# A selective scan in a hybrid layer stack: seven instead of five buffers for a step's feed and states

## The chip, the cores and the metric

The kernel runs on one core of a Trainium2 chip. The metric is the device time of one execution in microseconds (us): 3016.0 us, the median of three runs (3014.9 to 3018.98).

## What is computed

Four layers on x of shape (8, 512, 512): a selective scan (Mamba-like), a mixture of experts with a shared expert, causal attention, and a mixture of experts again. The change lies in the first one. Cut to it, the reference is

```python
xz = jnp.einsum('bld,kd->blk', x, W_x)             # x: layer-normed, 8 x 512 x 512
dt_raw, b_ssm, c_ssm = xz[..., :128], xz[..., 128:144], xz[..., 144:]
dt = jax.nn.softplus(jnp.einsum('blr,dr->bld', dt_raw, W_dt) + b_dt)
d_a = jnp.exp(dt[..., None] * a[None, None])       # 16 states for each channel
dbx = dt[..., None] * b_ssm[:, :, None, :] * x[..., None]
def step(h, inp):
    da_t, dbx_t, c_t = inp
    h = da_t * h + dbx_t
    y = jnp.einsum('bdn,bn->bd', h, c_t)
    return (h, y)
```

and after all four layers, each added to its input, the sum is the output. The experts' layer takes for each of 4096 tokens the best 6 of 64 experts, where an expert serves at most its first 64 tokens, and adds a shared gated expert of width 704.

## The kernel before

Everything is in float32. The five engines' programs are written from one plan, a list of items such as ("feed", k); each engine goes through the list and issues what is its own, so the order on an engine is that of the plan, and semaphores join the engines. Four stages follow each other: the scan (0 to about 1060 us), the first experts, attention, and the second experts.

**The scan stage.** One batch element has 512 time steps, which lie along the free axis, and 512 channels in four blocks of 128 partitions. A *step* k is one channel block and two of the 16 states (NG = 2): 32 steps a batch element, 256 in all (NSTEP). A step goes through the engines like this:

- `feed(k)`, POOL (GpSimd), L1872: writes dt*x*B for both states into buffer `hb[k % HB]`, 128x1024.
- `decay(k)`, ACT (ScalarE), L1720: writes exp(dt*a), one 128x512 tile for each state, into one of three PSUM banks.
- `scan(k)`, DVE (VectorE): two scans of 512 elements at L1349, then the product of the second state with C at L1358. In every eighth step (k % 8 == 4) DVE makes the first state's product too, L1355.
- `weigh_c(k)`, POOL, L1880: the product of the first state with C, in place in `hb`; left out in every eighth step.
- `sum(k)`, PE (TensorE), L1004: eight transposing 128x128 products add the step to y in a PSUM bank and signal `y_summed`. From then on `hb[k % HB]` is free.
- `x1(b, c)`, DVE, L1364: adds a finished y bank to x; it stands in the plan two steps after the block's last step, so it comes twice in a row every 16 steps.

The plan's order in step k is feed(k + 2), scan(k), weigh_c(k), x1 of step k - 2 where due, the work beside, sum(k - 1). AHEAD = 2 says how far the feeds run in front. C and B come from DRAM through three rotating buffers (NBC = 3, `bc_in`), broadcast to all partitions.

**The work beside.** In the same steps stand the preparation of the next batch element (norm, transposes, projections, softplus) and, for the batch element before, the first experts' norm, gate and routing and its shared expert: `sg` (L1054 on PE), `su` (L1075), `silu` (ACT, L1747), `hid` (DVE, L1377), `sd` (L1089 and L1095 on PE, L1392 on DVE). The products of PE go through a ring of three PSUM banks. An `sg` or `su` is one block of PE work that stands in front of a `sum` on PE's queue.

**The ring of buffers.** A feed may write its buffer when the step that used it last is summed:

```python
        if k >= HB:
            G.wait_ge(p.y_summed, k - HB)
        nc.gpsimd.tensor_tensor(out=p.hb[k % HB], ...)
```

With HB = 5 and the feed of step k + 2 standing in step k, POOL waits in step k until PE has summed step k - 3. What stands behind it on POOL's queue is weigh_c(k).

**The memory.** All tiles are cut by hand out of one SBUF tensor, `arena`, of ARENA words a partition. `hb` is the last part of `scan_memory`; the first experts' weights lie over the scan's tiles, and what lies behind starts at the end of `hb`. In front of `arena` lies the scratch in which the descriptors of DMAs issued by POOL are built. POOL issues these: 64 gathers (L1938), 64 accumulating writes of expert rows (L1948), and 12 accumulating writes of the shared expert (L1921), all behind the scan stage.

Of the kernel before, what the change touches and what calls it, by code (L numbers as in the profile page):

```python
# [33 lines left out]
NEG = -1e30  # L34
SCALE = float(1.0 / np.sqrt(np.float32(HEAD)))
BANK = 512
ARENA = 52928

# [3 lines left out]
GROUPS = NSTATE // NG  # L44
STEPS = GROUPS * HC
NSTEP = BATCH * STEPS
HB = 5
BOTH_EVERY, BOTH_AT = 8, 4
NBC = 3
AHEAD = 2  # L50
# [112 lines left out]
class Arena:  # L163
# [3 lines left out]
    def cut(self, shape, dt=FP32):  # L167
        n = int(np.prod(shape))
        words = n if dt in (FP32, I32) else (n + 1) // 2
        words = (words + 7) // 8 * 8  # L170
        assert self.at + words <= ARENA, (self.at, words)
        view = self.base[:, self.at:self.at + words]
# [30 lines left out]
def over(ap, axis, n):  # L203
    v = ap.unsqueeze(axis)
    shape = list(v.shape)
    shape[axis] = n
    return v.to_broadcast(shape)


def step_of(k):  # L210
    b, i = divmod(k, STEPS)
    pair, i = divmod(i, 2 * GROUPS)
    g, c = divmod(i, 2)
    return b, 2 * pair + c, g


def dve_weighs_both(k):
    return k % BOTH_EVERY == BOTH_AT
# [11 lines left out]
def block_of(ring, b, c):  # L230
    return half_of(ring, b, c // 2)[:, c % 2, :]
# [368 lines left out]
class Program:  # L600


    def __init__(self, nc, ctx, dram):
        self.nc, self.ctx, self.d = nc, ctx, dram
        self.signals = []
        base = ctx.enter_context(nc.sbuf_tensor("arena", [P, ARENA], FP32))
        self.bank = [ctx.enter_context(nc.psum_tensor(f"bank{i}", [P, BANK], FP32)) for i in range(8)]
# [117 lines left out]
    def scan_memory(self, sb):  # L725
# [10 lines left out]
        self.bc = [sb.cut([2, NG, SEQ]) for _ in range(NBC)]  # L736
        self.hb = [sb.cut([NG, SEQ]) for _ in range(HB)]

# [203 lines left out]
def tensor_engine(p, eng):  # L942
# [44 lines left out]
    def y_sum(k):  # L987
        b, c, g = step_of(k)
        s, w, each = b % 2, p.hb[k % HB], b * HC + c
        y = bank[Y_BANKS[c % 2]]  # L990
# [282 lines left out]
def vector_engine(p, eng):  # L1273
# [68 lines left out]
    def scan(k):  # L1342
        b, c, g = step_of(k)
        h = p.hb[k % HB]
        banks, both = [bank[p.da_bank(k, n)] for n in range(NG)], dve_weighs_both(k)
# [479 lines left out]
def pool_engine(p, eng):  # L1825
# [40 lines left out]
    def feed(k):  # L1866
        b, c, g = step_of(k)
        G.wait_ge(p.dtx_ready, b, c // 2)
        G.wait_ge(p.bc_in[k // 2 % NBC], k // 2)
        if k >= HB:  # L1870
            G.wait_ge(p.y_summed, k - HB)
        nc.gpsimd.tensor_tensor(out=p.hb[k % HB], in0=over(block_of(p.dtx, b, c), 1, NG), in1=p.bc[k // 2 % NBC][:, 0],  # L1872
                                op=ALU.mult).then_inc(*p.fed.up(k))
# [382 lines left out]
```

## Time and profile before

| | us |
|---|---|
| median of three runs | 3016.0 |
| the profiled execution | 3015.6 |
| its span on the core | 3013.8 |
| around the span | 1.8 |
| scan stage, to the last scan step's x1 | about 1060 |

The profile is of one execution. It gives each engine's busy time, what ended each idle stretch of an engine (the releaser), and the instructions in order of time. A stall of an engine that is not the last link costs nothing by itself. The rows that matter stand below, in groups.

### The profile page before, as it was taken

What the parts mean: (1) busy time and instruction counts of PE and PEld (TensorE: products, weight loads), DVE (VectorE), ACT (ScalarE), POOL (GpSimd) and SP (SyncE); (2) the same over time, 40 slices, a digit from 0 to 9 for tenths busy, and PEclk for the clock granted to TensorE, in tenths of its full rate; (3) what the DMA queues carried; (4) which work ended last, traced back from release to release, by engine and by line L of the source; (5) the groups of instructions that cost most, each with busy time, mean ns of one, the idle gap of its engine ahead of it and who ended that gap; (6) DMA issues with size and microseconds to landing.
All of it is one profiled execution on the core that took longest, in us unless ns stands there. A gap on an engine that the chain in (4) does not pass through costs nothing.

```text
span 3013.8 us, 37461 instructions
## 1 busy us (share of the span) xinstructions
PE 2720.2 (90%) x13484; PEld 1435.0 (48%) x13484; DVE 1772.6 (59%) x3835; ACT 1281.5 (43%) x2693; POOL 1483.1 (49%) x912
## 2 busy tenths in 40 slices
PE   4668888988889879999969999999899999999998
PEld 3454555545555534433335555555544444444443
DVE  5898999999899952222236666665624444222222
ACT  4657566665756411111127676666712220111111
POOL 5999989988998802222135555554500001121211
PEclk7779999999999889999989999999999999999999
DMA  5454555545554369999940000001135324899997
GB/s 187 153 184 154 185 167 166 187 142 195 166 176 164 131 265 358 396 393 393 392 121 1 29 29 29 29 29 42 64 100 189 118 79 159 308 381 338 359 337 218
DMA packets 168234, 566.13 MB, mean 188 GB/s; under 512 B 22832, under 2 KB 24752, under 8 KB 167536
## 3 DMA queue, kind: packets, MB, share of 16 engines
q1 hardware_dynamic: 149904, 521.65, 47.0%
q0 software_dynamic: 17088, 40.90, 5.9%
q8 instruction: 106, 1.74, 0.2%
q10 hardware_dynamic: 1056, 1.18, 0.1%
q14 instruction: 80, 0.66, 0.1%
HBM read 487.89 MB, written 75.79 MB: 187 GB/s over the span
## 4 chain that ended last, share of the span: by engine, by line
PE 53%; DVE 3%; ACT 2%; POOL 2%; DMA 2%; issue 1%; POOLq 0%; SPq 0%; DVEq 0%; ACTq 0%
PE bank L1151 10%; PE bank L1054 5%; PE bank L1075 5%; PE bank L1177 5%; PE bank L1089 5%; PE bank L1202 5%; PE bank L1259 4%; PE bank L1236 3%; PE bank L1224 2%; PE bank L1248 2%; POOL arena L1970 2%; DMA scratch_y<-arena 2%; PE bank L1134 1%; PE bank L1190 1%; ACT arena L1791 1%
## 5 line engine op out<-in xcount | busy, mean ns | idle before, releaser
L1872 POOL TENSOR_TENSOR arena<-arena 128x1024 f32<-128x1024 f32 x256 | 603.9, 2363 | 55.7 <-PE bank L1004 50.4
L1720 ACT ACTIVATE bank<-arena 128x512 f32<-128x512 f32 x512 | 344.5, 689 | 345.2 <-DVE arena L1349 184.7
L1970 POOL TENSOR_TENSOR arena<-arena 128x2048 f32<-128x2048 f32 (+3 forms) x128 | 296.9, 2323 | 275.0 <-DVE arena L1584 274.9
L1004 PE MATMUL bank<-arena 128*128 128x128 f32 x2048 | 296.7, 299 | 104.7 <-POOL arena L1880 103.5
L1791 ACT ACTIVATE arena<-arena 128x256 f32<-128x256 f32 (+3 forms) x512 | 287.1, 565 | 148.6 <-DVE arena L1575 124.9
L1349 DVE TENSOR_TENSOR_SCAN bank<-bank,arena 128x512 f32<-128x512 f32 x288 | 344.7, 1207 | 1.6 <-ACT bank L1720 1.1
L1004 PEld LDWEIGHTS bank<-arena 128*128 128x128 f32 x2048 | 258.0, 154 | 179.7 <-POOL arena L1880 128.5
L1151 PE MATMUL bank<-arena 128*64 128x352 f32 x2048 | 323.8, 470 | 0.0
L1054 PE MATMUL bank<-arena 128*128 128x512 f32 x640 | 298.2, 610 | 18.7 <-DVE arena L1377 18.7
L1075 PE MATMUL bank<-arena 128*128 128x512 f32 x640 | 288.7, 594 | 6.7 <-DVE arena L1339 6.7
L1880 POOL TENSOR_TENSOR arena<-arena 128x512 f32<-128x512 f32 x224 | 286.5, 1279 | 4.7 <-DVE arena L1349 4.5
L1349 DVE TENSOR_TENSOR_SCAN arena<-bank,arena 128x512 f32<-128x512 f32 x224 | 271.8, 1213 | 27.2 <-POOL arena L1872 14.5
L1089 PE MATMUL bank<-arena 128*128 128x512 f32 x640 | 286.5, 599 | 0.0
L1938 POOL DMA_INDIRECT arena<-scratch_xn,arena x64 | 68.7, 1073 | 440.8 <-DVE arena L1543 242.4
L1575 DVE CUSTOM_DVE_ANT_0 arena<-bank,arena 128x256 f32<-128x256 f32 (+3 forms) x512 | 220.9, 487 | 23.7 <-PE bank L1224 15.8
L1151 PEld LDWEIGHTS bank<-arena 128*64 128x64 f32 x2048 | 143.5, 139 | 147.6 <-issue 143.6
L1516 DVE TENSOR_TENSOR arena<-arena,bank 128x352 f32<-128x352 f32 x64 | 33.3, 521 | 306.9 <-issue 178.6
L1377 DVE TENSOR_TENSOR arena<-arena,bank 128x512 f32<-128x512 f32 x80 | 54.7, 683 | 244.5 <-PE bank L1075 243.7
L1075 PEld LDWEIGHTS bank<-arena 128*128 128x128 f32 x640 | 120.4, 190 | 160.2 <-issue 144.7
L1780 ACT ACTIVATE arena<-bank,arena 128x512 f32<-128x512 f32 x64 | 44.0, 687 | 346.7 <-PE bank L1177 324.2
L1054 PEld LDWEIGHTS bank<-arena 128*128 128x128 f32 x640 | 119.5, 195 | 149.9 <-issue 128.8
L1765 ACT ACTIVATE arena<-bank 128x352 f32<-128x352 f32 x64 | 29.7, 464 | 374.7 <-PE bank L1151 362.4
(145 smaller groups left out, 4187.9 us busy)
## 6 DMA issues: line engine op xcount, KB each, us to landing
arena<-scratch_bc SPq DMA_DIRECT2D x128, 1024.0 KB, 5.5
arena<-in_w_out SPq DMA_DIRECT2D x128, 768.0 KB, 15.3
arena<-in_w_gate SPq DMA_DIRECT2D x128, 704.0 KB
arena<-in_w_up SPq DMA_DIRECT2D x128, 704.0 KB
scratch_x<-arena SPq DMA_DIRECT2D x16, 1024.0 KB, 4.7
scratch_xn<-arena SPq DMA_DIRECT2D x15, 1024.0 KB, 4.6
arena<-scratch_x SPq DMA_DIRECT2D x44, 256.0 KB, 6.2
arena<-scratch_x SPq DMA_DIRECT2D x8, 1024.0 KB, 7.5
```

The costliest lines, as they stand in the source:

```text
L1004: i = nc.tensor.matmul(y[:, t * P:(t + 1) * P], w[:, n, t * P:(t + 1) * P], p.ident, is_transpose=True, start=False, stop=g == GROUPS - 1 ...
L1054: i = nc.tensor.matmul(out[:, :], f["swg"][:, c, j * P:(j + 1) * P], xnT[:, c, :], start=c == 0, stop=c == HC - 1)
L1075: i = nc.tensor.matmul(out[:, :], f["swu"][:, c, j * P:(j + 1) * P], xnT[:, c, :], start=c == 0, stop=c == HC - 1)
L1089: nc.tensor.matmul(out[:, :], f["shT"][:, j, t * P:(t + 1) * P], f["swd"][:, j, :], start=j == 0, stop=False)
L1151: i = nc.tensor.matmul(bank[1 + w][mine, 0:INTER], f["xeT"][k % 2][:, c, mine], f["ring"][(2 * k + half) % nw][w][:, c, :], start=c == 0, ...
L1349: nc.vector.tensor_tensor_scan(out=banks[n][:, :] if n or both else h[:, n, :], data0=banks[n][:, :], data1=h[:, n, :], initial=0.0, op0=A ...
L1575: nc.vector.tensor_tensor_reduce(out=p.sc[i % NSC][:, 0:width], in0=bank[c][:, 0:width], in1=p.amask[:, SEQ - width:], scale=-SCALE, scala ...
L1720: nc.scalar.activation(bank[p.da_bank(k, n)][:, :], block_of(p.dt, b, c), ACT.Exp, scale=p.alog[:, c, state:state + 1]).then_inc(*p.decaye ...
L1791: nc.scalar.activation(p.pr[n % 2][:, c, OFFSET[t]:OFFSET[t] + width], p.sc[i % NSC][:, 0:width], ACT.Exp, scale=-1.0, bias=p.nb[:, k % 2, ...
L1872: nc.gpsimd.tensor_tensor(out=p.hb[k % HB], in0=over(block_of(p.dtx, b, c), 1, NG), in1=p.bc[k // 2 % NBC][:, 0], op=ALU.mult).then_inc(*p ...
L1880: nc.gpsimd.tensor_tensor(out=h, in0=h, in1=p.bc[k // 2 % NBC][:, 1, 0, :], op=ALU.mult).then_inc(*p.weighted["pool"].up(k))
L1970: nc.gpsimd.tensor_tensor(out=own, in0=own, in1=over(p.rden[:, k % 2, :], 2, width), op=ALU.mult).then_inc(*p.divided.up(k))
```

## The change

`HB` goes from 5 to 7, and so does the distance in `feed`'s wait. Two buffers of 128x1024 words are 2048 words a partition more, so `ARENA` grows by 2048 words (8192 bytes). The descriptors' scratch is set to 8192 bytes a partition; it was not given before, and its default is 16384. With it `arena` begins 8192 bytes lower. AHEAD and NBC stay.

```diff
-ARENA = 52928
+ARENA = 52928 + 2048
+DYNAMIC_SCRATCH = 8192
...
-HB = 5
+HB = 7
...
-    nc = bacc.Bacc("TRN2", target_bir_lowering=False, num_devices=1)
+    nc = bacc.Bacc("TRN2", target_bir_lowering=False, num_devices=1, dynamic_dma_scratch_size=DYNAMIC_SCRATCH)
```

No instruction moves on any engine and none is added. What changes is in the waits. POOL's queue at the beginning of the scan steps, feeds (128x1024) and weighings (128x512) with the semaphores each waits on, of the kernel before:

```order
L1872 TENSOR_TENSOR arena<-arena 128x1024 [waits bc_in2]
L1880 TENSOR_TENSOR arena<-arena 128x512 [waits scanned]
L1872 TENSOR_TENSOR arena<-arena 128x1024 [waits y_summed]
L1880 TENSOR_TENSOR arena<-arena 128x512 [waits scanned]
L1872 TENSOR_TENSOR arena<-arena 128x1024 [waits y_summed,bc_in0]
L1872 TENSOR_TENSOR arena<-arena 128x1024 [waits y_summed]
```

and the same place with the change (lines are one further down):

```order
L1873 TENSOR_TENSOR arena<-arena 128x1024 [waits bc_in2]
L1881 TENSOR_TENSOR arena<-arena 128x512 [waits scanned]
L1873 TENSOR_TENSOR arena<-arena 128x1024
L1881 TENSOR_TENSOR arena<-arena 128x512 [waits scanned]
L1873 TENSOR_TENSOR arena<-arena 128x1024 [waits bc_in0]
L1873 TENSOR_TENSOR arena<-arena 128x1024 [waits y_summed]
```

The first feed that waits for a sum is the eighth, not the sixth, and each later one waits for a sum that lies two steps further back.

## Rows read from the trace of the kernel before

**Rows 1.** The page: the span, and part 1, busy us of each engine.
```profile
span 3013.8 us, 37461 instructions
PE 2720.2 (90%) x13484; PEld 1435.0 (48%) x13484; DVE 1772.6 (59%) x3835; ACT 1281.5 (43%) x2693; POOL 1483.1 (49%) x912
```

**Rows 2.** Busy time by stretches of the scan stage: length, PE, PEld, DVE, ACT, POOL, granted clock, DMA.
```profile
75.00:175.00 100.00, 57.99 (x287) 44.07 (x286) 88.25 (x99) 57.67 (x85) 99.38 (x62) 0.70 0.47 160
175.00:1020.00 845.00, 733.95 (x3352) 450.18 (x3351) 797.74 (x1060) 540.78 (x801) 767.27 (x456) 0.94 0.52 171
1018.00:1025.00 7.00, 6.12 (x14) 3.54 (x15) 6.86 (x7) 2.83 (x5) 6.87 (x5) 0.51 0.56 193
1025.00:1060.00 35.00, 34.55 (x141) 19.84 (x140) 25.82 (x30) 17.56 (x22) 23.59 (x14) 1.00 0.17 60
```

**Rows 3.** DVE's two largest waits, 175 to 1060 us: us, times, longest.
```profile
DVE arena L1364 <- PE bank L1004: 27.8, 8, 8.5
DVE arena L1349 <- ACT bank L1720: 12.4, 13, 2.0
```

**Rows 4.** DVE's waits for feeds, 0 to 175 us.
```profile
DVE arena L1349 <- POOL arena L1872: 14.5, 10, 4.9
```

**Rows 5.** POOL's waits before feeds, 75 to 1020 us.
```profile
POOL arena L1872 <- PE bank L1004: 49.2, 27, 4.2
POOL arena L1872 <- DMA arena<-scratch_bc: 2.0, 6, 0.5
```

**Rows 6.** Timeline around 284 and 415 us: start, us, instruction, [idle before <- releaser].
```profile
284.58 0.69 DVE L1364 TENSOR_TENSOR arena<-arena,bank 128x512 f32<-128x512 f32 x1 [3.01 <-PE bank L1004]
...
396.37 0.68 DVE L1377 TENSOR_TENSOR arena<-arena,bank 128x512 f32<-128x512 f32 x1
397.10 3.54 PE L1054 MATMUL bank<-arena 128*128 128x512 f32 x4 [2.67 <-DVE arena L1377]
...
413.37 1.91 PE L1004 MATMUL bank<-arena 128*128 128x128 f32 x16
414.56 2.36 POOL L1872 TENSOR_TENSOR arena<-arena 128x1024 f32<-128x1024 f32 x1 [4.22 <-PE bank L1004]
415.32 0.69 DVE L1364 TENSOR_TENSOR arena<-arena,bank 128x512 f32<-128x512 f32 x1 [4.42 <-PE bank L1004]
```

**Rows 7.** POOL's timeline, last quarter of the last batch element.
```profile
974.53 2.36 POOL L1872 TENSOR_TENSOR arena<-arena 128x1024 f32<-128x1024 f32 x1 [1.61 <-PE bank L1004]
980.84 2.35 POOL L1872 TENSOR_TENSOR arena<-arena 128x1024 f32<-128x1024 f32 x1 [2.72 <-PE bank L1004]
988.08 2.38 POOL L1872 TENSOR_TENSOR arena<-arena 128x1024 f32<-128x1024 f32 x1 [1.35 <-PE bank L1004]
...
1017.56 1.26 POOL L1880 TENSOR_TENSOR arena<-arena 128x512 f32<-128x512 f32 x1
1030.75 2.36 POOL L1872 TENSOR_TENSOR arena<-arena 128x1024 f32<-128x1024 f32 x1 [1.14 <-PE bank L1004]
```

**Rows 8.** DVE's timeline: scans of steps 242 and 245, and the first of the last x1.
```profile
1004.82 1.21 DVE L1349 TENSOR_TENSOR_SCAN arena<-bank,arena 128x512 f32<-128x512 f32 x1
...
1014.28 1.21 DVE L1349 TENSOR_TENSOR_SCAN arena<-bank,arena 128x512 f32<-128x512 f32 x1
...
1058.97 0.69 DVE L1364 TENSOR_TENSOR arena<-arena,bank 128x512 f32<-128x512 f32 x1 [8.48 <-PE bank L1004]
```

**Rows 9.** PE's timeline, the last 40 us of the scan stage.
```profile
1018.88 1.97 PE L1004 MATMUL bank<-arena 128*128 128x128 f32 x8 [3.72 <-POOL arena L1880]
1020.64 5.73 PE L1054 MATMUL bank<-arena 128*128 128x512 f32 x8
...
1029.63 2.78 PE L1004 MATMUL bank<-arena 128*128 128x128 f32 x24
...
1041.48 1.09 PE L1004 MATMUL bank<-arena 128*128 128x128 f32 x8 [0.45 <-POOL arena L1880]
```

**Rows 10.** DMAs issued by POOL: the page's queue, gathers' landing, first experts' row writes.
```profile
q0 software_dynamic: 17088, 40.90, 5.9%
```
```profile
DMA to landing us min/median/max: 6.6/7.1/11.2
```
```profile
L1948 POOL DMA_INDIRECT scratch_y<-arena x32: 1542/1587/1623, 1149.9 to 1522.0; - x32
```

## The prediction

> **What bounds the kernel now.** I read the page's first part, then the windows of the scan stage, the waits of DVE and of POOL in it, and the timelines at the stalls. PE is busy for 90% of the span and DVE for 59% [rows 1], but those are means over four stages, and only the first has the ring that is changed. In it, from 175 to 1020 us, DVE is busy for 797.74 of 845 us, 94%; POOL for 767.27, 91%; PE for 733.95, 87% [rows 2]. So DVE sets the pace, and what a change can give is what DVE idles. From 175 to 1060 us it idles before L1364, the x1, for a sum of PE (27.8 us, 8 times, the longest 8.5) and before its scans for a decay of ACT (12.4 us, 13 times) [rows 3]. No wait of DVE for a feed stands in that list. DVE waits for feeds earlier, 14.5 us up to 175 us [rows 4], where POOL is busy for 99.38 of 100 us [rows 2]: there POOL has too much work and does not wait for PE at all.
>
> POOL's wait for the ring is real: 49.2 us, 27 times, before a feed, for PE's sums [rows 5]. The question is whether anything that DVE waits for stands behind it.
>
> **The change part by part.** *The ring of seven.* The wait before a feed is for the sum five steps ahead of the one in hand, not three. A step takes about 4.1 us: the x1 stalls at 284.58 and 415.32 [rows 6] are one batch element apart, 130.7 us for 32 steps. So PE may fall behind by some 8 us more before POOL stops. The longest stall is 4.2 us [rows 5], so I take all 49.2 us as gone, and ask place by place who profits.
>
> First, the feeds themselves. They are two steps ahead of DVE and DVE waits for none of them after 175 us: 0 us.
>
> Second, weigh_c, which stands behind the feed on POOL, and through it PE's sums and then x1. DVE's stalls at x1 are eight, 27.8 us; the longest, 8.5 us, and one of 0.2 right behind it end the stage, and the six others, 19.1 us, look alike. At 415 us: `hid` ends on DVE at 396.37 + 0.68, and PE, which waited 2.67 us for just that, starts an sg at 397.10 [rows 6]. From there PE has work without a stop, sg, su and sums, and reaches the sum that x1 waits for at 413.37; DVE has stood for 4.42 us then, and POOL for 4.22 [rows 6]. Both wait for the same late PE. PE's row of work starts at an instant that DVE sets, so an earlier POOL moves nothing: x1 is as late as before. Only POOL's part of the double stall goes, and POOL then stands at weigh_c or the next feed, for DVE. The same holds at 284.58 (3.01 us) [rows 6] and at the other four: in each the last stop of PE ahead of its row of work is for DVE. 0 us of 19.1.
>
> Third, ACT's decays (12.4 us): the two largest kinds, 2.0 and 1.3 us, come where ACT has a softplus and a table change between decays. ACT waits for POOL there in no row: 0 us.
>
> Fourth, the end of the stage. The last stall at x1 is 8.48 us [rows 8], and here PE's row of work starts after a wait for POOL: 3.72 us at 1018.88 and 0.45 us at 1041.48, both for weigh_c; in between and behind PE is busy for 34.55 of 35 us [rows 2, 9]. PE was last held by POOL, so here POOL's delay counts. How much? POOL was stopped at 974.53, 980.84 and 988.08 for 1.61 + 2.72 + 1.35 = 5.68 us [rows 7], and from 988.08 to 1018.9 it never idles, so it carries a lag. It can lose that lag only down to DVE's scan. The weighing of step 242 can start when the scan does end, at 1004.82 + 1.21 = 1006.03 [rows 8]. From there POOL has a feed, a weighing and two feeds to the weighing of step 245: with 1.22 us from start to start for a weighing and 2.32 for a feed, 1006.05 + 1.22 + 2.32 + 1.22 + 2 x 2.32 = 1015.45. The scan of step 245 ends at 1014.28 + 1.21 = 1015.49 [rows 8]. So that weighing starts at about 1015.51 and not at 1017.56 [rows 7]: PE goes on 2.05 us earlier. The 5.68 us of stops are more than the lag that is to be lost, also with the earlier weighings held by their scans. At 1030.75 another stop of 1.14 us goes [rows 7], so the weighing that PE awaits at 1041.48 comes 2.05 + 1.14 = 3.2 us earlier, and PE's 0.45 us there go too. Sum for PE, and for the last x1, since nothing else is in its way: 2.05 + 0.45 = **2.5 us**. What follows (the last routing, the first gathers, the weights' loads, which wait for the last sum) starts from there and moves along.
>
> Bounds: if the clock does better the rest comes with it. PE's sg after the 3.72 us wait took 5.73 us for 8 products [rows 9] at a granted 0.51 [rows 2], the level of 1.2 GHz, against 3.60 for the same block at full level. With a shorter wait the level may stay up; then POOL's weighing of 1041 is the limit, and the gain 3.3 us. Above all stands the stall of 8.48 us [rows 8], which can't go twice. Below, 0, if PE meets the lower level elsewhere.
>
> *The bc loads.* Their buffers are given back by POOL's and DVE's weighings, not by PE. POOL waits 2.0 us for them in 945 us [rows 5]; some of POOL's gain may turn into this wait, which costs no one (same reason as above).
>
> *The scratch.* The software queue moves 17088 packets [rows 10] in 140 DMAs, 122 each. They all come after the scan stage, and a gather lands in 7.1 us, 11.2 at most [rows 10]. A gather is issued three expert pairs ahead of its use, and a pair takes (1522.0 - 1149.9)/31 = 12.0 us [rows 10]. If half the scratch held only one DMA at a time, the second and third gather at the start would land later by about 6 and 12 us; at 12 us a pair that is in time. I take 0 us. The Trainium skill bears on this ("DMA: Bandwidth & Descriptors", Terms, and The descriptor swizzle): a descriptor is 16 bytes in a ring in SBUF, and a transfer to 128 partitions takes 9 on each side for each engine. By that page 8192 bytes hold 512, an estimated 56 transfers; no row here shows a ring's fill. By the page the sum is the same 0, so the rule speaks for the cut, not against it.
>
> *The addresses.* All tiles lie 8192 bytes lower or, behind `hb`, where they lay. No row shows a time that depends on an address: 0 us.
>
> The sum: against the profiled execution 3015.6 - 2.5 = 3013.1, against the median 3016.0 - 2.5 = **3013.5 us**.
>
> **The rivals.** *More than the end is gained.* If PE's earlier sums do reach the x1 stalls of the middle, up to 19.1 us more go [rows 3], 3016 - 2.5 - 19.1 = 2994; with ACT's 12.4 too, 2982. For it: 49.2 us of POOL's stops go, and POOL is at 91%. Against it: in rows 6 PE waits for DVE, not for POOL, ahead of the late sum. From the second of the stalls on it is more than 0.2%.
>
> *Nothing arrives.* The ring is longer, but AHEAD = 2 and NBC = 3 are not, and the last stretch of PE comes as late as before because a wait for DVE takes the place of that for POOL at 1018.88: 3016.0. For it: DVE's scan of step 245 ends only 2.07 us before the weighing starts. Against it: 2.05 us are left even so.
>
> *Slower, by PE's clock.* PE's waits and rows of work shift by 2 to 4 us in each half of a batch element. Where a stretch at the lower level falls on the sg and su ahead of an x1, DVE's stall is 4.42 instead of 3.01 us [rows 6], 1.41 more; in the trace one of the six is so long. And a stretch like that at 1018 us costs a block 5.73 - 3.60 = 2.13 us [rows 9]. If the other five had it and two blocks more at the end, 7.1 + 4.3 - 2.5 = 8.9, 3024.9; it decides for slower than 0.2% when nearly all of them have it. For it: the granted clock is 0.94 over the stage [rows 2], so low stretches are about; against it: a POOL that is late less often leaves PE fewer long waits.
>
> *Slower, by the scratch.* As above, only if a DMA's issue on POOL had to wait for more than a pair's time; each 1 us that a pair then lost would be 64 us. I see no row for it.
>
> **How the numbers follow.** 0.2%, 6 us, is about what a measurement of this kernel can tell from no change. The forecast, 2.5 us less (0 to 3.3 by its own bounds, up to 8.5 at the most), 0.70; nothing arrives 0.15; more in the middle 0.08; slower by the clock 0.05; by the scratch 0.02. The range reaches from 3016.0 - 8.5 = 3007.5 to the three runs' upper end and a little of the clock's rival, 3019.5. Faster by over 0.2%: 0.09; within: 0.85; slower: 0.06.
>
> **What would show it.** In the profile after, POOL's wait before L1873 for PE is nearly gone from 49.2 us; PE's wait for weigh_c (L1881) at about 1019 us is down from 3.7 to under 2 us; DVE's waits at x1 (L1365) keep their six of about 3 to 4.4 us, and the last falls from 8.48 to about 6. The waits up to 175 us stay. The stages behind keep their lengths. I am wrong if the x1 stalls of the middle shrink, if DVE had waited for POOL in a way the list puts down to another, or if POOL's gathers take longer to issue.

## The result

| | median us | runs | ratio to before, 95% interval |
|---|---|---|---|
| before | 3016.1 | 6 | |
| seven buffers | 3026.8 (3024.8 to 3030.9) | 6 | 1.0035 (1.0023 to 1.0048) |

The change makes the kernel slower, by 10.7 us. Forecast were 3013.5 us, and 0.06 for slower.

The page of the kernel after, the span and part 1, which answer to [rows 1]:

```profile
span 3025.6 us, 37460 instructions
PE 2719.3 (90%) x13484; PEld 1432.7 (47%) x13484; DVE 1786.5 (59%) x3835; ACT 1281.5 (42%) x2693; POOL 1483.8 (49%) x912
```

DVE makes the same 3835 instructions, and is busy for 13.9 us more (1786.5 against 1772.6). The other engines are within 1 us of before. That is the first thing to see: DVE's waits in the scan stage didn't grow, its instructions got longer. Lines in the kernel after are one further down: L1873 is the feed, L1881 the weighing, L1350 the scans, L1365 the x1.

POOL's waits from 75 to 1020 us, against [rows 5] (waited for: us, times, longest):

```profile
POOL arena L1881 <- DVE arena L1350: 42.9, 52, 2.3
POOL arena L1851 <- DVE arena L1311: 34.4, 10, 5.5
```

and in the kernel before, the same two:

```profile
POOL arena L1850 <- DVE arena L1310: 18.7, 10, 2.9
POOL arena L1880 <- DVE arena L1349: 4.5, 12, 0.7
```

The 49.2 us for PE are gone altogether, as they should be. In their place POOL waits for DVE's scans, 42.9 us (4.5 before), and for DVE's norm sums, 34.4 us (18.7 before). POOL lags much less behind DVE. Worked out from the two traces, 175 to 1020 us, a weighing starts 2.35 us (median) after the scan that it waits for has ended in the kernel before, and 0.75 us after it in the kernel with seven; it starts within 0.1 us of the scan's end in 15 of 184 cases before and 75 of 182 after. DVE's wait for PE from 175 to 1060 us, against [rows 3]; its wait for ACT is 12.8 us and was 12.4:

```profile
DVE arena L1365 <- PE bank L1005: 17.7, 6, 3.0
```

With the last x1, which now lies at 1066 us, DVE's waits at x1 are 24.6 us over the whole run and were 28.6. So waits gave back 4.0 us, instructions took 13.9, and the stretch from the first x1 to the last, 101.3 to 1059.8 us before, is 98.6 to 1067.1 us after: 958.5 and 968.5 us, 10.0 more. The profiled run of after reaches the first x1 2.7 us earlier than that of before, the last one 7.3 us later, and its end 11.8 us later. So 4.5 us more came up behind the scan stage. PE is busy for 3.7 us more in the experts' products (L1152, 327.5 us, L1151 before 323.8), which may be part of them, but that isn't shown. The medians differ by 10.7 us, about the stage's 10.0; the 4.5 us of this one pair of profiled runs stay unexplained.

**Which instructions.** Among DVE's groups three grew, all of the experts' routing, which runs beside the scan. They negate the row maximum (L1415), multiply the scores with the inverse of their sum (L1424), and compare to make the mask (L1444). The groups of DVE of before, then those of after (xcount | busy us, mean ns | idle before):

```profile
L1423 DVE TENSOR_TENSOR arena<-arena 128x256 f32<-128x256 f32 x16 | 9.8, 615 | 0.5
L1443 DVE TENSOR_SCALAR arena<-arena 128x256 f32<-128x256 f32 x16 | 8.4, 528 | 0.6
L1414 DVE TENSOR_SCALAR arena<-arena 128x4 f32<-128x4 f32 x16 | 6.7, 420 | 0.6
```
```profile
L1444 DVE TENSOR_SCALAR arena<-arena 128x256 f32<-128x256 f32 x16 | 15.4, 960 | 0.6
L1424 DVE TENSOR_TENSOR arena<-arena 128x256 f32<-128x256 f32 x16 | 14.7, 922 | 0.5
L1415 DVE TENSOR_SCALAR arena<-arena 128x4 f32<-128x4 f32 x16 | 8.6, 536 | 0.6
```

7.0 + 4.9 + 1.9 = 13.8 us: all of DVE's growth between these two profiles. Each kernel has one profile, and the size leans on which one is compared: against the two kernels below that wait as with five buffers (e1_wait5 and e2_scratch, DVE busy 1776.9 and 1776.7 us) the growth is 9.6 and 9.8 us. Seven of each sixteen run in the scan stage. The shortest, the median and the longest of the same lines' sixteen (ns), in the trace of before and then of after:

```profile
L1414 DVE TENSOR_SCALAR arena<-arena x16: 169/170/1103, 199.0 to 2477.4; 128x4 f32<-128x4 f32 x16
L1423 DVE TENSOR_TENSOR arena<-arena x16: 425/425/2474, 209.6 to 2479.3; 128x256 f32<-128x256 f32 x16
L1443 DVE TENSOR_SCALAR arena<-arena x16: 293/295/1745, 219.7 to 2483.5; 128x256 f32<-128x256 f32 x16
```
```profile
L1415 DVE TENSOR_SCALAR arena<-arena x16: 170/172/2345, 196.2 to 2489.3; 128x4 f32<-128x4 f32 x16
L1424 DVE TENSOR_TENSOR arena<-arena x16: 425/426/2619, 206.8 to 2491.2; 128x256 f32<-128x256 f32 x16
L1444 DVE TENSOR_SCALAR arena<-arena x16: 293/295/2420, 216.9 to 2495.4; 128x256 f32<-128x256 f32 x16
```

An instruction of one shape that takes 293 ns or 1745 ns is being held. This stood in the trace of before, and the prediction did not look at it.

**By what.** The mask's comparison of the same quad (one batch element's four row tiles; seven quads are routed beside the scan), DVE's timeline with POOL's beside it. Before, DVE then POOL (start us, us):

```profile
345.69 0.67 DVE L1443 TENSOR_SCALAR arena<-arena 128x256 f32<-128x256 f32 x1
```
```profile
344.93 1.28 POOL L1880 TENSOR_TENSOR arena<-arena 128x512 f32<-128x512 f32 x1
346.16 2.41 POOL L1872 TENSOR_TENSOR arena<-arena 128x1024 f32<-128x1024 f32 x1
```

After, DVE then POOL:

```profile
342.57 2.42 DVE L1444 TENSOR_SCALAR arena<-arena 128x256 f32<-128x256 f32 x1
```
```profile
341.26 1.27 POOL L1881 TENSOR_TENSOR arena<-arena 128x512 f32<-128x512 f32 x1
342.49 2.35 POOL L1873 TENSOR_TENSOR arena<-arena 128x1024 f32<-128x1024 f32 x1
```

In both cases DVE's operation ends 0.15 us after the POOL instruction that was running when it began: 346.36 after 346.21, 344.99 after 344.84. Before, the comparison comes 0.76 us after the weighing has begun and waits for its tail. After, POOL is half a microsecond earlier against DVE: the comparison comes 1.31 us after the weighing's start, so the weighing is over, the feed has begun 0.08 us before, and the comparison waits for nearly all of its 2.35 us. In six of the seven quads of before the comparison waits for a weighing and takes at most 0.69 us; after, in six of seven it waits for a feed and takes 1.6 to 2.4 us.

The first operation shows the same at 983 us of the kernel after, with a tensor of four elements a partition, DVE then POOL:

```profile
983.37 2.35 DVE L1415 TENSOR_SCALAR arena<-arena 128x4 f32<-128x4 f32 x1
```
```profile
983.34 2.35 POOL L1873 TENSOR_TENSOR arena<-arena 128x1024 f32<-128x1024 f32 x1
```

It also goes the other way round. In the kernel before, a product and a weighing begin together, and this time the weighing is the longer one, 1.55 us where its median is 1.27:

```profile
471.72 0.42 DVE L1423 TENSOR_TENSOR arena<-arena 128x256 f32<-128x256 f32 x1
```
```profile
471.72 1.55 POOL L1880 TENSOR_TENSOR arena<-arena 128x512 f32<-128x512 f32 x1
```

### The profile page after: what moved, and what is told of

It reads as the page before. It is cut to its first block, busy times and chain, and to the rows that moved or that the text cites. A ratio compares the mean times of both kernels' runs of the same rounds, so it can differ in the third digit from the quotient of the medians.

```text
span 3025.6 us, 37460 instructions
## 1 busy us (share of the span) xinstructions
PE 2719.3 (90%) x13484; PEld 1432.7 (47%) x13484; DVE 1786.5 (59%) x3835; ACT 1281.5 (42%) x2693; POOL 1483.8 (49%) x912
## 4 chain that ended last, share of the span: by engine, by line
PE 51%; DMA 4%; DVE 3%; ACT 3%; POOL 2%; issue 1%; POOLq 0%; SPq 0%; DVEq 0%; ACTq 0%
PE bank L1152 9%; PE bank L1055 5%; PE bank L1076 5%; PE bank L1178 5%; PE bank L1203 5%; PE bank L1090 5%; PE bank L1260 4%; PE bank L1237 3%; DMA scratch_y<-arena 3%; PE bank L1225 2%; PE bank L1249 2%; POOL arena L1971 2%; PE bank L1135 1%; PE bank L1191 1%; ACT arena L1792 1%
## 5 line engine op out<-in xcount | busy, mean ns | idle before, releaser
L1873 POOL TENSOR_TENSOR arena<-arena 128x1024 f32<-128x1024 f32 x256 | 603.1, 2362 | 10.6 <-DMA arena<-scratch_bc 6.8
L1350 DVE TENSOR_TENSOR_SCAN bank<-bank,arena 128x512 f32<-128x512 f32 x288 | 344.7, 1207 | 1.6 <-ACT bank L1721 1.1
L1152 PE MATMUL bank<-arena 128*64 128x352 f32 x2048 | 327.5, 474 | 0.0
L1055 PE MATMUL bank<-arena 128*128 128x512 f32 x640 | 294.5, 604 | 18.7 <-DVE arena L1378 18.7
L1881 POOL TENSOR_TENSOR arena<-arena 128x512 f32<-128x512 f32 x224 | 285.3, 1274 | 45.7 <-DVE arena L1350 45.0
L1350 DVE TENSOR_TENSOR_SCAN arena<-bank,arena 128x512 f32<-128x512 f32 x224 | 271.8, 1213 | 27.4 <-POOL arena L1873 14.4
L1152 PEld LDWEIGHTS bank<-arena 128*64 128x64 f32 x2048 | 144.6, 140 | 150.2 <-issue 146.1
```

Source lines behind the costliest of these rows:

```text
L1055: i = nc.tensor.matmul(out[:, :], f["swg"][:, c, j * P:(j + 1) * P], xnT[:, c, :], start=c == 0, stop=c == HC - 1)
L1152: i = nc.tensor.matmul(bank[1 + w][mine, 0:INTER], f["xeT"][k % 2][:, c, mine], f["ring"][(2 * k + half) % nw][w][:, c, :], start=c == 0, ...
L1350: nc.vector.tensor_tensor_scan(out=banks[n][:, :] if n or both else h[:, n, :], data0=banks[n][:, :], data1=h[:, n, :], initial=0.0, op0=A ...
L1881: nc.gpsimd.tensor_tensor(out=h, in0=h, in1=p.bc[k // 2 % NBC][:, 1, 0, :], op=ALU.mult).then_inc(*p.weighted["pool"].up(k))
```

## The experiments

Theory A is that of the rows above: the three operations can't run while an instruction of POOL on SBUF tensors runs, and the ring of seven puts POOL's feeds where they come. Theory B: the lower addresses or the halved scratch slow DVE. Each line gives the median of several runs. The experiments ran on three chips, each beside the kernel before, whose medians were 3016.8 us (e1 to e4), 3016.9 (e5 to e8) and 3015.6 (e9 and e10); the ratios are to these. DVE busy and the stage are those of one profiled run for each kernel. "Stage" is the stretch from the first x1 to the last.

| kernel | median us | ratio to before (95%) | DVE busy | stage |
|---|---|---|---|---|
| before | 3016.1 | | 1772.6 | 958.5 |
| after | 3026.8 | 1.0035 (1.0023 to 1.0048) | 1786.5 | 968.5 |
| e1_wait5 | 3016.7 | 0.9997 (0.9988 to 1.0006) | 1776.9 | 961.6 |
| e2_scratch | 3016.7 | 1.0001 (0.9991 to 1.0010) | 1776.7 | 961.3 |
| e3_yield7 | 3010.0 | 0.9979 (0.9970 to 0.9989) | 1768.9 | 952.8 |
| e4_noport7 | 3008.8 | 0.9974 (0.9965 to 0.9983) | 1765.9 | 949.0 |
| e5_yield5 | 3016.0 | 0.9996 (0.9987 to 1.0005) | 1776.0 | 960.1 |
| e6_noport5 | 3008.4 | 0.9975 (0.9964 to 0.9985) | 1766.4 | 951.6 |
| e7_six | 3026.1 | 1.0028 (1.0017 to 1.0040) | 1785.0 | 970.0 |
| e8_mixed7 | 3005.3 | 0.9971 (0.9961 to 0.9981) | 1765.0 | 949.8 |
| e9_mask7 | 3019.7 | 1.0015 (1.0007 to 1.0024) | 1776.0 | 960.5 |
| e10_mixed5 | 3011.4 | 0.9985 (0.9976 to 0.9994) | 1766.9 | 955.5 |

**The wait alone, the memory alone.** e1_wait5, against the changed kernel:

```diff
-        if k >= HB:
-            G.wait_ge(p.y_summed, k - HB)
+        if k >= 5:
+            G.wait_ge(p.y_summed, k - 5)
```

> The changed kernel with its seven buffers, its addresses and its halved scratch, but a feed waits for the sum of step k - 5 as before. Theory A (contention): DVE's three routing operations (the negation of the row maximum, the product with the inverse, the comparison that makes the mask) use something of SBUF that POOL's feeds use too; with the longer distance POOL no longer stands still for PE when they come, and DVE busy in the scan stage grew by 13.8 us. Then this kernel takes 3016 us (3013 to 3019) and DVE is busy for 1772 us. Theory B (memory): the lower addresses or the smaller scratch slow DVE; then it takes 3027 us and DVE is busy for 1786 us.

e2_scratch, against the kernel before:

```diff
+DYNAMIC_SCRATCH = 8192
...
-    nc = bacc.Bacc("TRN2", target_bir_lowering=False, num_devices=1)
+    nc = bacc.Bacc("TRN2", target_bir_lowering=False, num_devices=1, dynamic_dma_scratch_size=DYNAMIC_SCRATCH)
```

> The kernel before with the descriptors' scratch halved and nothing else: five buffers, and all of the tiles 8192 bytes lower. Theory A: 3016 us, and the 140 DMAs that POOL issues take as long to issue and land as before (1.07 us, 7.1 us). Theory B: above 3020 us, and if it is the scratch, in the experts' stages.

Both are the kernel before again: 3016.7 us. Theory B falls, and the cut of the scratch costs nothing that can be measured; a gather still takes 1.07 us to issue and 7.0 to land. DVE busy is 4 us above the profile of before, where theory A had 1772: the product's group takes 12.9 us here and 9.8 there. The addresses need not be the reason, since e5_yield5, with the scratch and the addresses of before, has 12.6 us. How the operations fall between POOL's instructions may shift from run to run, but no kernel has a second profile that would show it.

**Keep POOL away.** e3_yield7, against the changed kernel, on POOL:

```diff
+    def yield_to(m, q, part):
+        if m == 0 and q < BATCH - 1:
+            G.wait_ge(p.routed, m, q, part)
+    def route_max(m, q):
+        yield_to(m, q, "less")
+    def route1(m, q):
+        yield_to(m, q, "score")
+    def masks(m, q):
+        yield_to(m, q, "mask")
...
```

> The changed kernel, and POOL waits in the scan stage at each of the three routing operations of DVE until DVE has made it (21 waits, no instruction more). Theory A: the operations fall to their undisturbed 0.17, 0.42 and 0.29 us, DVE busy falls by about 24 us to 1762, POOL loses some 1 to 2 us at each wait, which the longer ring and its 43 us of waiting for DVE cover; time 3003 to 3009 us, faster than both kernels. Theory B: a POOL that waits more can only cost: 3027 us or more.

3010.0 us: 17 us less than the changed kernel, 7 less than before, though all that was added is waits. The mask's comparison, in the trace of this kernel:

```profile
L1444 DVE TENSOR_SCALAR arena<-arena x16: 293/294/295, 219.1 to 2477.4; 128x256 f32<-128x256 f32 x16
```

None of the sixteen is held any more; with seven buffers and no waits the longest took 2420 ns. DVE busy went to 1768.9, not to 1762: a wait keeps POOL from starting what stands behind it, but not from being in the middle of something when the operation comes. The first product still took 3.7 us, and four of the seven negations 0.9 us or more. That product is longer than any feed: POOL was in a feed when it came (207.48 to 209.88 us), went on with the weighing behind it, and the product ended 0.28 us after the weighing.

**Give DVE a form that is not held.** e4_noport7, against the changed kernel (shown for the comparison; the negation is written likewise, the product becomes four such, with the inverse as a scalar of each row tile, and `arena` grows by 16 words for the sums):

```diff
+        if m == 0 and q < BATCH - 1:
+            nc.vector.tensor_scalar(f["mask"][s], marked[:, :, 0:E], -2.0, None, ALU.is_equal, ALU.add,
+                                    accum_out=f["junk"][:, 4:5]).then_inc(*p.routed.up(m, q, "mask"))
+            return
```

> The changed kernel, and in the scan stage the three routing operations are written in the form of tensor_scalar that also gives a sum (the product with the inverse as four of them, one for each row tile), so that each has one tensor input and, by theory A, needs nothing that POOL holds. They get longer by themselves: some 0.8 us more for each of seven quads, 6 us. Theory A: the operations show one duration each in the whole stage, DVE busy falls by 24 - 6 us, time 3008 to 3014 us. Theory B: 3027 + 6 = 3033 us.

3008.8 us. The comparison and the reading of its sum, in the trace of this kernel:

```profile
L1456 DVE TENSOR_SCALAR_CACHE_REDUCE arena<-arena x7: 419/420/422, 217.0 to 990.4; 128x256 f32<-128x256 f32 x7
L1456 DVE DVE_READ_ACCUMULATOR arena<-arena x7: 82/83/84, 217.4 to 990.7; 128x1 f32 x7
```

419 to 422 ns in all seven places, beside the same POOL. By itself the form is slower than the 293 ns of the old one, but nothing holds it. The sum's reading overlaps its end: together they keep DVE busy for 3.0 us in the seven places, 0.43 us each. The seven quads' products take 6.2 us in all, by the same count, and the negations 1.15 us. The Trainium skill ("SBUF — State Buffer", Who interferes with whom) tells this rule: VectorE's second pair of SBUF ports is GpSimd's too, it is held for a whole instruction by whoever starts first, and on VectorE it is wanted by a tensor_scalar or copy between SBUF tensors in its fast mode and by an operation with two SBUF inputs, but not by the form of tensor_scalar with a sum. The trace agrees where this kernel has the case: the two kinds of tensor_scalar and the product with two SBUF inputs are held (up to 2420, 2345 and 2619 ns), the form with a sum isn't (419 to 422 ns), and POOL's weighing is held when the product came first (1.55 us at 471.72). No run here tests a copy, nor shows the fast mode as such. That it is this port, and not something else that POOL holds, only the page says.

**Is it the waits or the ring?** e5_yield5 is the kernel before with the waits of e3_yield7; against that one (`arena` and the scratch are those of before):

```diff
-HB = 7
+HB = 5
```

> The kernel before (five buffers) with POOL's 21 waits of e3_yield7 alone. If the waits are what pays (theory A), the comparison falls to its 0.29 us here too and DVE busy to about 1768 us; the time is 3010 to 3014 us, since POOL, which still stops 49 us for PE, has less to spare. If the longer ring is what pays (theory D), 3017 us or more, since POOL's lag grows and DVE waits for feeds.

3016.0 us, no gain, and no loss either. Theory A had DVE busy at 1768 us and the time at 3010 to 3014; DVE busy is 1776.0, so the waits alone did not do it. Theory D (the longer ring is what pays) had 3017 or more, which is within the noise of 3016.0. With five buffers POOL is more often inside an instruction when DVE comes, so waiting at the next one is too late: of the seven places each, all negations, six products and five comparisons are still held, against six, one and none in e3_yield7. In this trace the comparison still takes up to 1.8 us:

```profile
L1443 DVE TENSOR_SCALAR arena<-arena x16: 293/294/1786, 217.7 to 2482.4; 128x256 f32<-128x256 f32 x16
```

So the waits keep POOL away only where POOL lags little, which is what the longer ring gives. In time, the two ratios' intervals (0.9970 to 0.9989 and 0.9987 to 1.0005) overlap slightly.

**What is the ring worth where nothing is held?** e6_noport5 is the kernel before with the operations of e4_noport7; against that one (`arena` and the scratch are those of before, plus the 16 words):

```diff
-HB = 7
+HB = 5
```

> The kernel before (five buffers) with the three operations in the form of e4_noport7. It measures what the ring of seven is worth where nothing collides. Theory A with the prediction's sum: DVE busy 1766 us as in e4_noport7, and 2.5 to 4 us more time than that kernel, 3011 to 3013 us. If the ring is worth nothing by itself: 3009 us, the time of e4_noport7.

3008.4 us, the time of e4_noport7: by the medians the ring is worth nothing by itself. With e4_noport7 this also settles the cause: the three operations as they were, two more buffers cost 10.7 us; the three operations rewritten, they cost nothing that can be measured (0.9974 against 0.9975 of the kernel before, each to within 0.001). So the loss goes through these operations. The stages of the two profiled runs differ by 2.6 us (951.6 and 949.0), and so do their spans (3007.8 and 3005.2), which is the size of the prediction's 2.5; but single runs of either kernel spread by 8 us and more, so it stays open whether those 2.6 us are real.

**Six buffers.** e7_six, against the changed kernel:

```diff
-ARENA = 52928 + 2048
-DYNAMIC_SCRATCH = 8192
-HB = 7
+ARENA = 52928 + 1024
+DYNAMIC_SCRATCH = 12288
+HB = 6
```

> Six buffers instead of seven, the scratch at 12288 bytes. Theory A: what counts is whether POOL still stands still for PE when the operations come; the stalls of the kernel before are up to 4.2 us and a step is 4.1 us, so nearly all go with one buffer more already, and time and DVE busy are those of the changed kernel, 3024 to 3027 us and 1786 us. If each buffer adds its part: 3021 us.

3026.1 us and DVE busy 1785.0: the loss of seven buffers is there with one buffer more (1.0028, 1.0017 to 1.0040). In its profile POOL hardly waits for PE and waits for DVE as long as with seven:

```profile
POOL arena L1881 <- DVE arena L1350: 42.4, 53, 2.3
POOL arena L1873 <- PE bank L1005: 4.5, 4, 1.4
```

A weighing starts 0.77 us (median) after its scan's end, as with seven (0.75). The sixth buffer does it, and the seventh adds nothing that can be measured.

**One operation alone.** e9_mask7 is the changed kernel with only the comparison rewritten, as in the diff of e4_noport7:

```diff
+        if m == 0 and q < BATCH - 1:
+            nc.vector.tensor_scalar(f["mask"][s], marked[:, :, 0:E], -2.0, None, ALU.is_equal, ALU.add,
+                                    accum_out=f["junk"][:, 0:1]).then_inc(*p.routed.up(m, q, "mask"))
+            return
```

> The changed kernel with the comparison that makes the mask, and only that of the three, in the form with a sum. In the changed kernel's trace the seven comparisons of the scan stage take 12.7 us; in this form each takes 0.42 and 0.08 for the sum's reading, 3.5 us. Theory A: 9 us less if the other two collide as before, 3017 to 3019 us; less of a gain, 3019 to 3023 us, if a DVE that is earlier runs into a feed at one of the other two instead. Theory B is gone.

3019.7 us: 7 us of the loss came back, a little less than the 9 of the first case, and the 2 us between are less than the noise. DVE busy fell by 10.5 us. The product and the negation have the same sums as in the changed kernel, 14.6 and 8.3 us (14.7 and 8.6), but not by staying as they were. With the comparison rewritten, the products at 334 and 596 us take 2.54 us each (0.43 in the changed kernel), and those of the quads at about 732 and 861 us fall from 2.62 and 2.54 to 0.43. Which of them is held is a matter of where the two engines' queues happen to stand; that the sums came out the same is luck.

**Both remedies together.** e8_mixed7 has the rewritten negation and comparison, and for the product POOL's wait; e10_mixed5 is the same with five buffers. e8_mixed7, against e4_noport7 (in which the product was four operations with a sum), on POOL:

```diff
+    def route1(m, q):
+        if m == 0 and q < BATCH - 1:
+            G.wait_ge(p.routed, m, q, "score")
```

and e10_mixed5, against e8_mixed7 (`arena` and the scratch are those of before, plus the 16 words):

```diff
-HB = 7
+HB = 5
```

> Seven buffers; the negation and the comparison in the form with a sum, as in e4_noport7, and for the product with the inverse a wait of POOL, as in e3_yield7, with the operation as it was. Theory A: 7 x (4 x 0.358 - 0.425) = 7 us less of DVE than e4_noport7, of which a collision of the first product takes 3 back: DVE busy 1762 us, time 3004 to 3007 us.

> The fastest so far, e8_mixed7, with five buffers and the scratch as before: what the ring of seven is worth in it. With the prediction's 2.5 us: 3007 to 3009 us. If POOL's wait at the product needs the longer ring to be covered: 3010 us or more. If the ring is worth nothing: 3005 us.

e8_mixed7 takes 3005.3 us, 11.6 less than before beside it and 21 less than the changed kernel. It has the lowest median, but it isn't shown to be the fastest: five of its eleven runs lie between 3008.4 and 3014.5, and its interval (0.9961 to 0.9981) covers the ratios of e4_noport7 (0.9974) and of e6_noport5 (0.9975), which has five buffers. DVE busy is 1765.0 and not 1762. The expectation added up 0.358 us for each of the four operations, but they overlap and take 6.2 us in seven quads, 0.89 a quad; the one product takes 4.3 us here, so only 1.9 us could go.

With five buffers it is 3011.4 (4.2 less than before). The intervals of the two ratios overlap (0.9961 to 0.9981, and 0.9976 to 0.9994), so the times alone don't decide. The stages, 949.8 and 955.5 us, and the product's group, 8.1 and 10.8 us, point the same way as the medians and as e3_yield7 beside e5_yield5: where POOL is to make way, the longer ring helps.

## Why the prediction was wrong, by its own steps

- *DVE sets the pace of the stage.* Right: in the two profiles DVE's instructions took 13.8 us more, its waits at x1 4.0 less, and the stage grew by 10.0.
- *POOL's 49.2 us of waiting for PE go.* Right, all of them.
- *The x1 stalls of the middle stay, since PE's row of work starts after a wait for DVE.* Right: six waits of 3.0 us at most, 17.7 us in all. They were 19.1; the one of 4.42 us is 3.0 now.
- *The end of the stage: PE starts 2.05 us earlier at the sum of step 245, and the last stall of 8.48 us gets shorter.* The first term is right, the second isn't, and the sum comes out partly by luck. PE's timeline of the kernel after:

```profile
1027.00 1.17 PE L1005 MATMUL bank<-arena 128*128 128x128 f32 x8 [1.70 <-POOL arena L1881]
1028.00 3.60 PE L1055 MATMUL bank<-arena 128*128 128x512 f32 x8
```

  The wait was 3.72 us and is 1.70 [rows 9], 2.02 less. The block behind it takes 3.60 us and no longer 5.73, since the granted clock is 1.00 from 1027 to 1034 us; it was 0.51 at this block in the kernel before [rows 2]. The last stall, DVE's timeline of after:

```profile
1066.22 0.69 DVE L1365 TENSOR_TENSOR arena<-arena,bank 128x512 f32<-128x512 f32 x1 [5.87 <-PE bank L1005]
```

  5.87 us where it was 8.48: 2.6 us shorter, forecast 2.5. But the term of 0.45 us, PE's wait for the weighing of 1041.48, did not go:

```profile
1038.09 1.09 PE L1005 MATMUL bank<-arena 128*128 128x128 f32 x8 [1.31 <-POOL arena L1881]
1048.73 1.09 PE L1005 MATMUL bank<-arena 128*128 128x128 f32 x8 [0.93 <-POOL arena L1881]
```

  PE, earlier by 2.0 us and by the 2.13 us of the faster block, waited 2.24 us for two weighings instead. That is the prediction's own bound for a clock that stays up, where POOL's weighings are the limit. From the end of the scan of step 245 to the last x1 it is 43.5 us before and 40.6 after.

- *The scratch and the addresses cost nothing.* Right, by e1_wait5 and e2_scratch. The sign "the stages behind keep their lengths" is off by 4.5 us in this pair of profiles, and why stays open.
- *What failed is the frame of the sum,* the step "what a change can give is what DVE idles". The prediction asked "who profits" from a POOL that stops less, and put down 0 where no one waited for it. It took every duration on DVE as fixed and let only waits change. The term that is missing, put at nothing without a reason, is what POOL's instructions, once they start elsewhere, do to the instructions beside them: 7.0 + 4.9 + 1.9 = 13.8 us on DVE in the two profiles (9.6 us against e1_wait5). The bound of "below, 0" was no bound for the same reason. The rival "slower, by PE's clock" had the direction but not the cause: PE's busy time fell by 0.9 us.
- Could it have been seen? Yes, in the trace of before: mean durations of 528 and 615 ns over minima of 293 and 425 ns for the same shape, on the engine that sets the pace. The price could have been estimated: seven quads, three operations, each held for about a feed at worst, 21 x 2.36 = 50 us above nothing, of which 24.9 - 16 x (0.17 + 0.425 + 0.295) = 10.7 us were paid already. The direction of the whole could not be read from the rows, but a place at risk could. The feed that POOL starts late at 974.53 [rows 7] has 0.43 us left when this negation comes, which so takes 0.46 us:

```profile
976.46 0.46 DVE L1414 TENSOR_SCALAR arena<-arena 128x4 f32<-128x4 f32 x1
```

  Without the stop of 1.61 us that feed starts at 972.92, the weighing behind it at 975.24 and the next feed at 976.46, by the prediction's own 2.32 and 1.22 us: the instant at which the negation comes. In the kernel after, feed and negation do meet there, and it takes 2.35 us (983.37, above).

## What to carry to other kernels

Read a line's least and greatest duration, not only its mean, on the engine that sets the pace: where one shape takes 0.3 or 1.7 us, look at what the other engines run at that moment, since a change that moves their instructions can move that too. Before a buffer is added to take away a stall of POOL, rewrite the operations that are held. Here the longer ring lost 10.7 us alone; with the three operations rewritten it lost nothing and won nothing that could be measured, and the rewriting by itself, with five buffers, gained 8 us.

## What the runs showed of the hardware

- A DVE tensor_scalar between SBUF tensors (128x256 or 128x4) and a tensor_tensor with two SBUF inputs (128x256) end 0.15, 0.03 and 0.28 us after the POOL instruction that held them; undisturbed they take 0.29, 0.17 and 0.42 us, held up to 2.4, 2.3 and 3.7 us (the 3.7 behind a feed and the weighing after it). The profile books this as the instruction's own time, not as a wait. A fourth operation is held in the same way outside the scan stage: after it, twelve of DVE's tensor_scalars of the norm (L1325, 128x512, undisturbed 0.54 us) take 0.72 to 2.75 us, each ending 0.28 us after a tensor_tensor of POOL, some 14 us too long together, the same before and after. What that costs in time is untested.
- The form of tensor_scalar that also gives a sum took 419 to 422 ns for 128x256 and 157 ns for 128x4 at any place. The reading of the sum, 82 ns, overlaps its end: the two together take 0.43 us for 128x256.
- DVE's scans and products with one SBUF and one PSUM input (L1350, L1359) kept their 1.21 and 0.69 us beside the same POOL instructions.
- A weighing of POOL (128x512, median 1.27 us) that began together with a product on DVE took 1.55 us.
- Half of the descriptors' scratch, 8192 bytes a partition, carried the 140 DMAs that POOL issues as before: 3016.7 us, and gathers issued in 1.07 us and landed in 7.0 (median).
